# Causal mask of the value pass: by TensorE for every second pair of heads, by GpSimd for the others

## What is computed

```python
def _L0_attn_ref(x, Wq, bq, Wk, bk, Wv, bv, Wm, bm):
    ...
    scores = jnp.einsum('bhqd,bhkd->bhqk', q, k) / SCALE
    causal_mask = jnp.arange(seq)[None, :] > jnp.arange(seq)[:, None]
    scores = jnp.where(causal_mask, jnp.float32(-1000000000000.0), scores)
    probs = jax.nn.softmax(scores, axis=-1)
    attn = jnp.einsum('bhqk,bhkd->bhqd', probs, v)
    ...

x = x + _L0_attn_ref(xn, ...) + _L0_ffn_ref(xn, ...)
x = x + _L1_attn_ref(xn, ...) + _L1_ffn_ref(xn, ...)
```

## Time and profile before

| what | value |
|---|---|
| median of 3 runs | 1815.94 us (1813.59 to 1822.41) |
| profiled execution, its own time | 1819.73 us |
| its span | 1818.0 us |
| mean granted TensorE clock | 0.943 of full |
| TensorE busy | 1599.6 us, 88% |
| VectorE busy | 1372.1 us, 75% |
| ScalarE busy | 947.3 us, 52% |
| GpSimd busy | 917.1 us, 50% |
| selects of GpSimd (line 1480) | 256, 175.3 us |
| fill products (line 934) | 1001 |

### The profile page before, as it was taken

One profiled execution on the slowest core, in us unless ns is written; L12 is line 12 of the kernel. 1 busy time (PEld: TensorE's weight loads), 2 busy tenths in 40 slices (PEclk: granted clock), 3 DMA queues, 4 the chain that ended last, 5 costly groups with the idle time before them and its releaser, 6 DMA issues. The chain is left out here.

```text
span 1818.0 us, 34322 instructions
## 1 busy us (share of the span) xinstructions
PE 1599.6 (88%) x12535; PEld 1107.9 (61%) x12537; DVE 1372.1 (75%) x2530; ACT 947.3 (52%) x1610; POOL 917.1 (50%) x960
## 2 busy tenths in 40 slices
PE   5979998879887889888888999999999999999982
PEld 4644455446455555444444777888888778877741
DVE  5868766557766767866576798788888899898983
ACT  5622566447555656445554445566655554655510
POOL 6236747553655356477678326642221355646055
PEclk9889999889888999989899999999999999999986
DMA  8963789779878766466436756876665778877432
GB/s 270 281 168 101 197 236 291 225 211 264 246 232 244 231 161 156 135 157 166 143 105 181 226 200 202 258 218 195 192 197 189 221 220 265 248 232 224 136 98 79
DMA packets 284392, 363.69 MB, mean 200 GB/s; under 512 B 32688, under 2 KB 213040, under 8 KB 278080
## 3 DMA queue, kind: packets, MB, share of 16 engines
q1 hardware_dynamic: 243168, 297.68, 56.8%
q0 software_dynamic: 17056, 33.66, 6.5%
q10 hardware_dynamic: 24000, 30.15, 4.8%
HBM read 207.51 MB, written 121.90 MB: 181 GB/s over the span
## 5 line engine op out<-in xcount | busy, mean ns | idle before, releaser
L1469 POOL DMA_INDIRECT xs_dram<-sc_in,pos x256 | 267.7, 1046 | 144.5 <-issue 66.6
L1443 POOL DMA_INDIRECT gat<-ys_dram,pos x256 | 271.8, 1062 | 120.7 <-issue 62.8
L2063 DVE TENSOR_REDUCE row_max<-R 128x6 f32<-128x768 f32 x256 | 239.8, 954 | 112.1 <-PE R L1015 55.5
L934 PE MATMUL R<-ident_b 128*128 128x512 bf16 x1001 | 281.1, 403 | 21.3 <-issue 4.0
L1480 POOL TENSOR_SCALAR_AFFINE_SELECT probs<-probs 128x512 f32<-128x512 f32 x256 | 175.3, 685 | 224.6 <-ACT probs L1641 219.7
L1641 ACT ACTIVATE probs<-R 128x768 f32<-128x768 f32 x256 | 203.6, 808 | 120.9 <-PE R L1039 95.0
L1158 PEld LDWEIGHTS Y<-fd,hid 128*128 128x128 f32 (+1 forms) x1680 | 221.2, 192 | 47.1 <-DVE hid L2213 18.7
L1158 PE MATMUL Y<-fd,hid 128*128 128x128 f32 (+1 forms) x1680 | 239.0, 280 | 10.3 <-DVE hid L2213 10.1
L1489 POOL TENSOR_TENSOR o_acc<-o_acc,read 128x512 f32<-128x512 f32 x98 | 128.0, 1306 | 215.0 <-DVE read L2170 213.6
L901 PE MATMUL R<-fhl,fw 128*128 128x512 f32 (+1 forms) x484 | 190.6, 394 | 1.6 <-issue 1.0
L934 PEld LDWEIGHTS R<-ident_b 128*128 128x128 bf16 x1001 | 93.0, 101 | 146.6 <-issue 55.0
(11 more groups left out here) (282 smaller groups left out, 3463.2 us busy)
## 6 DMA issues: line engine op xcount, KB each, us to landing
fw<-wf SPq DMA_DIRECT2D x44, 1408.0 KB
q_rows<-kq SPq DMA_DIRECT2D x128, 256.0 KB, 5.3
fx<-xs_dram SPq DMA_DIRECT2D x74, 256.0 KB
fd<-in_L_ffn_w_dram SPq DMA_DIRECT2D x44, 320.0 KB
xs_dram<-gat SPq DMA_DIRECT2D x24, 512.0 KB, 5.2
qk_dram<-qk_parts SPq DMA_DIRECT2D x32, 384.0 KB
Q<-qk_dram SPq DMA_DIRECT2D x64, 192.0 KB
K<-qk_dram SPq DMA_DIRECT2D x64, 192.0 KB
```

The source lines that it names most:

```text
L934: pe.matmul(psum["R"][:, b * C:(b + 1) * C], ident_b[:, :], ident_b[:, :].unsqueeze(1).to_broadcast([P, TILES, P]), start=True, stop=True)
L1443: pool.indirect_dma_start(gat[:, i % 2, 2 * t + a, :], None, ys_dram[l][g], bass.IndirectOffsetOnAxis(ap=pos[l][g][a][:, col:col + 1], axi ...
L1469: pool.indirect_dma_start(xs_dram[g], bass.IndirectOffsetOnAxis(ap=pos[l][g][a][:, col:col + 1], axis=0), sc_in[:, n % 2, t * P:(t + 1) * ...
L2063: dve.tensor_reduce(row_max[:, b, :, :, h2].rearrange("p c g -> p g c"), pair[:, :].rearrange("p (g c t) -> p g c t", g=2, t=P)[:, :, 0:3, :],
```

## The change

For an even pair k the mask is added to the scores in PSUM: two products of 128 x 256 with `causal` as weights and the identity as the moving operand add -1e30 where the key comes after the query, so that the exponential gives zero. The score products of those pairs leave their accumulation open. GpSimd's select remains for the odd pairs. The value product waits for the bank's release by the exponential where the mask was TensorE's, for the select where it was GpSimd's. Some target times of the table are moved with it, and the planner writes new orders.

```diff
+def masked_on(k):
+    return "PE" if k % 2 == 0 else "POOL"
...
-    f0 = [f0_start + 8.80 * f - 95.63 * (f >= NT[0][0]) for f in range(sum(NT[0]))]
+    f0 = [f0_start + 8.80 * f - 99.83 * (f >= NT[0][0]) for f in range(sum(NT[0]))]
...
-                stage(t, "B2", n, k, after=[(("BM", n, b, "SP"), 2.4), ("KC", 0, 0, "DVE")], PE=0.36,
-                      ACT=(0.7, [("BP", *divmod(i - 2, NPAIR // 2), "PE")] if i >= 2 else []), POOL=0.68)
+                free = [("BP", *divmod(i - 2, NPAIR // 2), "PE")] if i >= 2 else []
+                after = [(("BM", n, b, "SP"), 2.4), ("KC", 0, 0, "DVE")]
+                if masked_on(k) == "PE":
+                    stage(t, "B2", n, k, after=after, PE=0.58, ACT=(0.7, free))
+                else:
+                    stage(t, "B2", n, k, after=after, PE=0.36, ACT=(0.7, free), POOL=0.68)
...
-                    after = [("B2", n, k - 1, "POOL"), ("B2", n, k, "POOL"), ("Q4", n, 0, "ACT")]
+                    after = [("B2", n, i, "POOL" if masked_on(i) == "POOL" else "ACT") for i in (k - 1, k)] + [("Q4", n, 0, "ACT")]
...
-        c.append(max(hw(2 * n + 3.6) + 32.10, f0[sum(NT[0][:g + 1]) - 1] + 12.00, (c[-1] if c else 0) + 12.74))
+        c.append(max(hw(2 * n + 3.6) + 39.09, f0[sum(NT[0][:g + 1]) - 1] + 12.00, (c[-1] if c else 0) + 13.08))
...
-        t = max(b_end + -3.00, c_end[g] + 130.60, (f1[-1] if f1 else 0) + 23.24)
+        t = max(b_end + -3.00, c_end[g] + 130.60, (f1[-1] if f1 else 0) + 17.83)
...
-            t = max(f1[sum(NT[1][:g + 1]) - 1] + 76.50, d[n] + 56.00, t + 10)
+            t = max(f1[sum(NT[1][:g + 1]) - 1] + 79.44, d[n] + 56.67, t + 10)
...
-    route(1, 0, c_end[0] + -33.90)
+    route(1, 0, c_end[0] + -39.00)
     scatter(1, 0, c_end[0] + 66.83, 7.8)
-    route(1, 1, c_end[1] + -33.90)
+    route(1, 1, c_end[1] + -44.77)
...
+                    on_pe = masked_on(k) == "PE"
                     for g, bank in enumerate(banks):
                         pe.matmul(bank[:, 0:3 * P].rearrange("p (c t) -> p c t", t=P)[:, 0:3:2, :],
-                                  key[g][:, q0:q0 + P], q[g][:, q0:q0 + S], start=True, stop=True)
+                                  key[g][:, q0:q0 + P], q[g][:, q0:q0 + S], start=True, stop=not on_pe,
+                                  skip_group_check=True)
                     for g, bank in enumerate(banks):
                         ins = pe.matmul(bank[:, P:2 * P], key[g][:, q0 + P:q0 + S], q[g][:, q0 + P:q0 + S],
-                                        start=True, stop=True)
+                                        start=not on_pe, stop=not on_pe, skip_group_check=True)
+                    if on_pe:
+                        for bank in banks:
+                            ins = pe.matmul(bank[:, 0:2 * P].rearrange("p (c t) -> p c t", t=P), causal[:, :],
+                                            ident_b[:, :].unsqueeze(1).to_broadcast([P, 2, P]),
+                                            start=False, stop=True, skip_group_check=True)
                     ins.then_inc(pair.full, 1)
...
-                            wait(*probs_masked(n, 2 * k + c // 2 + 1))
+                            pair = 2 * k + c // 2
+                            if masked_on(pair) == "POOL":
+                                wait(*probs_masked(n, pair // 2 + 1))
+                            else:
+                                wait(*bank_of["st", n, pair].released())
...
-                if kind == "B2":
+                if kind == "B2" and masked_on(k) == "POOL":
```

More of the change, by code:

```diff
@@ L846, in two_layer_kernel @@
         max_split = signal("max_split")
-        probs_masked, values_weighted = signal("probs_masked", NPAIR), signal("values_weighted", 2 * GROUPS)
+        probs_masked, values_weighted = signal("probs_masked", NPAIR // 2), signal("values_weighted", 2 * GROUPS)
         b3_loaded, acc_saved = signal("b3_loaded", 2, 16), slots("acc_saved")
```

## The result

| | before | after |
|---|---|---|
| median of the runs of one comparison, us | 1819.18 (4 runs, 1813.59 to 1826.40) | 1909.43 (4 runs, 1907.38 to 1912.39) |
| profiled execution, span, us | 1818.0 | 1907.3 |

After to before is 1.0496, 95% interval 1.0458 to 1.0535. The change costs 5%, some 90 us, where the prediction had a gain of 12 and a range that ended at 1832.

What follows compares the result with a forecast made beforehand. It took TensorE's work list to bound the expert stretch, with GpSimd nearly full at the step before it. Terms +6 - 6 + 7 - 17 - 2 = -12 us gave 1804 us from 1816; range 1784 to 1832, the forecast's own 1793 to 1812.

Steps and rivals of the forecast that it cites:

- Term 2: Attention: taking half of the selects off GpSimd shortens the value product's waits, -6 us, bounds 0 and -25.8.
- Rival C: Attention's second half: GpSimd's queue held it back, so the change is much faster, about 1784 us; chance 0.11.
- term 3: Step from attention to experts: delta-chunk work moves ahead of the first expert tile, +7 us, bounds -7 and +26.
- Term 1: Attention, TensorE: mask products +27.5, fewer fills -28.8, steps out of the half array +8; sum +6 us, bounds -1 and +35.
- the +26: Attention, TensorE: alternative size of Term 1 if every one of the 128 masked pairs pays a tiling-mode step.
- Rival B: Attention: masks and steps are paid, fewer fills give nothing back, so slower, about 1833 us; chance 0.23.
- Terms 3 to 5: Behind the attention: step to the experts +7 us, expert stretch -17 us, tail -2 us.
- The expert stretch: Layer-1 experts, bound by TensorE: fewer fills, state products and other chunk products there, -17 us, bound 0.
- The tail: After the experts: fewer gathers ahead of the last chunk's rsqrt, -2 us, bounds -4 and +5.
- The signs that the prediction named: Wrong altogether if the first expert tile came after 1030 us or the attention's clock (420 to 650 us) fell below 0.91.

Runs made afterwards that it cites:

- E8: The kernel before with its own order, the even pairs' selects left out and nothing in their place: 1.0287 x before, +52 us.
- E10: Order of before, products for even pairs, GpSimd waiting as before and doing two needless memsets in each removed select's place: 1.0028 x before, +5 us.
- E4: The kernel before with its order, fills and constants, even pairs masked by the 256 products in place of selects: 1.0367 x before, +67 us.
- E3: The changed kernel with the 256 mask products left out, even pairs unmasked: 1.0430 x before, +78 us.
- E5: The kernel before with 130 of the attention's fill products not issued: 0.9947 x before, -10 us.
- E7: E4 with each mask made of four half-array products of 64 rows in place of two full-array ones: 1.0385 x before, +70 us.
- E6: The changed kernel with 128 more fill products in the attention: 1.0498 x before, +90 us.
- E15: The changed kernel with two needless GpSimd memsets at each of 219 places between neighbouring indirect DMAs of the attention: 0.9965 x before, -6 us.
- E16: The kernel before with two needless GpSimd memsets at each of 129 places between neighbouring indirect DMAs of the attention: 0.9777 x before, 1769.79 us.
- E1: The kernel before with only the seven moved constants of the planner's table, all masks still selects: 1.0157 x before, +29 us.
- E2: The changed kernel with the seven constants put back to their old values and the plan made anew: 1.0648 x before, +118 us.
- E9: E4 with GpSimd again waiting for the even pair's exponential where its select stood, doing no work there: 1.0169 x before, +31 us.

## Why the prediction was wrong

**Term 2 failed, "Half of the selects off GpSimd: -6 us in the attention", and its bounds "0 and -25.8".** It priced the select as work and as a wait, and both left: the value product waits no more. (The lower bound was too wide by itself: 9.2 of the 25.8 us are counted twice, and the wait was 16.6.) But the selects were also what kept GpSimd's indirect DMAs apart and in step with ScalarE. Measured alone (E8) the term is +52, on the side that the bounds shut out; given back (E10) it takes 62 of E4's 67 us away. I had asked what waits for GpSimd, not what GpSimd would start sooner. Rival C, "GpSimd's queue was what held the attention's second half back", was wrong in the same place. Its sum was wrong too: the 20 us of waiting and the 14 of term 3 at its lower end make 1770, not 1784.

**Term 1 came near in sum, by luck.** +6 was forecast for products, steps and fewer fills, and each part was mis-sized. The products, priced at 27.5, cost 5 us with GpSimd as before (E10, interval 0.5 to 9) and 12 to 15 in its denser state (E3, E4 less E8); 130 fills fewer brought 10 of their 28 us (E5). The counted step to the full array, 0.21 us, did not show as time: E7 avoids it, with twice the products, and gains nothing, and E10's 5 us hold the steps of 128 masked pairs. So the +26 was not seen either. The prediction worked it out from the rule of the Trainium skill, TensorEngine Tiling (Array Packing), Key Properties, that a change of tiling mode drains TensorE, and from the row's 0.21 us.

**Rival B had the right sign and place** (the attention, 1833) **and the wrong mechanism.** It said that the fills give nothing back and that masks lie on the path; E3 shows that without any mask product the changed kernel is still +78, and E10 that the products alone are +5.

**Terms 3 to 5.** The step to the experts was forecast at +7 and came to 40 - 30 = +10. The expert stretch was -17 and came to -10; the sum's 17 counted 35 fills fewer in full; that some of them had stood in waits and give nothing back is likely, and not tested. The tail was -2 and came to +3. With the attention's 87 that is 87 + 10 - 10 + 3 = 90, against 89.3 between the spans.

**The signs that the prediction named** did point there: the first expert tile after 1030 us (1105.91), and a clock in the attention below 0.91 (0.89). But the fills, to which it tied the clock, are not what the time hangs on: with 128 more the clock there rises from 0.89 to 0.92 and the time stays (E6), with 130 fewer it goes from 0.91 to 0.90 and the kernel is 10 us faster (E5). With the DMAs apart and only the change's fewer fills, E15 shows 0.96 from 420 to 650 us.

**The chances and the range.** 0.23 for slower rested on one rival, whose term was 35 us at most. A rival in which a freed engine does harm was missing. The forecast's own range, 1793 to 1812, is narrower than the bounds of terms 3 and 5 that it names, which add up to 1788 to 1830.

What stays open: by which way a run of indirect DMAs holds up TensorE's signals. The runs show that the time between their starts decides (1.26 us: late, 1.45: less, 1.8: next to none), that it needs them near, and that a busy DMA alone does not do it. Nothing here tells whether it is their descriptors, their transfers or their signals. Open are also the 34 us between E15 and E16. That the 29 us of the constants (E1) lie behind the attention is read off the trace: it ends at 977 us for 980, but the step to the experts takes 41 us for 30 and the tail 94 for 88. In E2, with the constants undone, that step takes 60 us where the change has 40.

## What to carry to other kernels

When an edit frees an engine, list what that engine will start sooner, and look beyond its own path: a wait or an instruction can be what keeps transfers apart (E8, E9). A wait that the profile cannot tie to an instruction, on consumers of TensorE whose product shows as done, is the sign; set such waits against the times of indirect DMAs. If they fall together, try a needless 0.3 to 0.65 us on GpSimd between neighbouring indirect DMAs, and stop before GpSimd becomes the bound.

## What the runs showed of the hardware

Unexpected were: that indirect DMAs of GpSimd 1.26 us apart delay the signals of TensorE products, in the place shown by 6 to 8 us and of products that read nothing of what was gathered, and that 1.8 us apart they do not (E15); that four signals held back in this way then came within 0.21 us; that work without use on one engine makes the kernel 2.2% faster (E16); and that TensorE's clock, 0.91 in the attention's middle before, rises to 0.96 with no fill product more, once the DMAs stand apart (E16).
